# Decoder kernel: norm powers in pairs of batches, transposed outputs copied from separate banks, two steps reordered

## The reference, cut to what matters

```python
x = layernorm(x + L0_attn(x))            # gated delta-rule linear attention, 16 heads of 8
x = layernorm(x + L0_xattn(x, ctx))      # cross attention on a strided gather of keys
x = layernorm(x + L0_ffn(x))             # relu(h + c * sin(theta + 0.1 h)), h = x W1 + b1
x = layernorm(x + L1_attn(x))            # selective scan, 256 channels, 16 states
x = layernorm(x + L1_xattn(ctx, x))      # cross attention, 8 heads of 128
x = layernorm(x + L1_ffn(x))             # receptance-gated feed-forward
```

## Time and profile before

| | before |
|---|---|
| median of 3 runs | 370.88 us (369.8 to 370.9) |
| the profiled execution's own time | 370.45 us |
| its span, first to last instruction | 368.6 us |
| mean granted TensorE clock | 0.952 |
| busy, share of the span: PE, DVE, ACT, POOL | 86%, 81%, 60%, 54% |
| DMA, mean over the span | 66 GB/s |

### The profile page before, as it was taken

One profiled execution on the slowest core, in us unless ns is written; L12 is line 12 of the kernel. 1 busy time (PEld: TensorE's weight loads), 2 busy tenths in 40 slices (PEclk: granted clock), 3 DMA queues, 4 the chain that ended last, 5 costly groups with the idle time before them and its releaser, 6 DMA issues. The chain is left out here.

```text
span 368.6 us, 5671 instructions
## 1 busy us (share of the span) xinstructions
PE 318.2 (86%) x1758; PEld 240.6 (65%) x1758; DVE 300.4 (81%) x739; ACT 222.7 (60%) x511; POOL 200.0 (54%) x236
## 2 busy tenths in 40 slices
PE   5858494997998999888868989898799989999993
PEld 2646393895665647743536955476599668989873
DVE  0798999996977889999999999999958534754945
ACT  4666323233265869887778628888555746775742
POOL 2399997664413141899999899868602800100111
PEclk9989599699999999989996998999999999999999
DMA  8910000000000003345443544444200000000011
GB/s 249 424 57 2 1 0 3 0 1 2 0 2 1 0 2 118 110 136 157 153 133 116 160 128 133 145 140 127 84 2 0 2 0 1 2 1 2 1 30 28
DMA packets 11525, 24.45 MB, mean 66 GB/s; under 512 B 1231, under 2 KB 2255, under 8 KB 11239
## 3 DMA queue, kind: packets, MB, share of 16 engines
q1 hardware_dynamic: 11495, 24.09, 20.0%
HBM read 23.50 MB, written 0.59 MB: 65 GB/s over the span
## 5 line engine op out<-in xcount | busy, mean ns | idle before, releaser
L1064 POOL TENSOR_TENSOR arena<-arena 128x512 f32<-128x512 f32 x63 | 80.0, 1280 | 25.8 <-DVE arena L716 24.0
L716 DVE TENSOR_TENSOR_SCAN arena<-arena,ps 128x512 f32<-128x512 f32 x64 | 77.3, 1209 | 0.1
L1344 ACT ACTIVATE arena<-arena,neg_a 128x508 f32<-128x508 f32 x64 | 43.9, 715 | 6.9 <-DVE arena L716 5.9
L1820 PE MATMUL ps<-first_in,arena 128*128 128x128 f32 x256 | 42.3, 291 | 3.0 <-POOL arena L1064 2.8
L709 DVE TENSOR_TENSOR ps<-arena,ps 128x512 f32<-128x512 f32 x64 | 43.2, 676 | 0.5 <-PE ps L1804 0.5
L1820 PEld LDWEIGHTS ps<-first_in,arena 128*128 128x128 f32 x256 | 33.3, 149 | 14.2 <-POOL arena L1064 8.1
L1110 POOL TENSOR_TENSOR rstd<-veps,mhalf 128x4 f32<-128x4 f32 (+2 forms) x6 | 5.0, 837 | 67.5 <-DVE veps L818 35.5
L744 DVE TENSOR_REDUCE arena<-ps 128x2 f32<-128x496 f32 x32 | 21.3, 667 | 24.8 <-PE ps L1866 24.8
L1804 PE MATMUL ps<-arena,pick_wide 96*128 96x512 bf16 x64 | 25.7, 407 | 12.6 <-DVE arena L716 12.2
L1633 PE MATMUL ps<-arena,first_in 128*128 128x128 f32 (+1 forms) x192 | 26.8, 305 | 8.8 <-POOL arena L941 8.8
L1633 PEld LDWEIGHTS ps<-arena,first_in 128*128 128x128 f32 x192 | 26.1, 219 | 11.0 <-POOL arena L941 10.3
(11 more groups left out here) (300 smaller groups left out, 792.4 us busy)
## 6 DMA issues: line engine op xcount, KB each, us to landing
arena<-c_rows_dram SPq DMA_DIRECT2D x64, 256.0 KB, 3.1
fold_in<-in_fold_dram SPq DMA_DIRECT2D x1, 2056.0 KB, 11.3
late_in<-in_late_dram SPq DMA_DIRECT2D x1, 1423.5 KB, 17.3
early_in<-in_early_dram SPq DMA_DIRECT2D x1, 921.5 KB, 13.1
xres<-in_x_dram SPq DMA_DIRECT2D x1, 512.0 KB, 13.9
kv_ctx<-in_context_dram SPq DMA_DIRECT2D x1, 480.0 KB, 7.1
first_in<-in_first_dram SPq DMA_DIRECT2D x1, 465.0 KB, 3.4
rows_in<-in_rows_dram SPq DMA_DIRECT2D x1, 384.0 KB, 14.4
```

Of the source, the lines that this page charges most:

```text
L716: nc.vector.tensor_tensor_scan(hist[:, q % NBUF], fade[:, q % NFADE], chain(q), 0.0, ALU.mult, ALU.add).then_inc(S("scan"), 1)
L1064: tt(seen[:, q % NBUF], hist[:, q % NBUF], c_wide[:, q % NBUF], ALU.mult).then_inc(S("read_out"), 1)
L1344: act(fade[:, q % NFADE].rearrange("p (b t) -> p b t", t=T)[:, :, 1:], dt[:, n, cols(g)].rearrange("p (b t) -> p b t", t=T)[:, :, 1:], ACT ...
L1820: ins = mm(y_bank(p // NS)[:, b * T:(b + 1) * T], seen[:, p % NBUF, b * T:(b + 1) * T], ident, is_transpose=True, start=False, stop=last a ...
```

## The change

Six edits.

1. In the norms (1, 0), (2, 0), (2, 1) and (3, 0), the list PAIRED, statistics, epsilon and power are done for two batches at a time: two "var" and two "rstd" counts a half, two powers of 128x2 in place of one of 128x4, and `norm_finish` waits for its pair's power.
2. The eight transposes of the linear attention's output go to bank 6 (blocks 0 to 3), bank 7 (4, 5) and bank 5 (6, 7). VectorE copies bank 6, ScalarE banks 7 and 5. All eight turns of `ot` follow when all three copies are in; they go to banks 4 to 7 by pairs of batches, and VectorE copies pairs 0 and 2, ScalarE pairs 1 and 3. `key_rows(0)` moves ahead of `landed(1, 0)`.
3. The subtraction of the maximum and the exponential of the first cross attention are split into two pairs of batches.
4. GpSimd's `power(2, 0)`, `residual_half(3, 0)` and `power(2, 1)` move ahead of the making of `s3_cf`; `power(3, 0)` moves ahead of `residual_half(3, 1)` and its wait.
5. In the sine stage `normal(3, 0, 0)` moves ahead of `last_fraction(1)`; on ScalarE the last block's sine moves behind the two copies to `xcol`.
6. Before the scan VectorE's subtraction for dt (L698) moves ahead of the three instructions for the low bits of B.

```diff
+        PAIRED = [(1, 0), (2, 0), (2, 1), (3, 0)]
+        def o_rows_bank(i):
+            return (bank(6)[:, i * P:(i + 1) * P] if i < 4 else bank(7 if i < 6 else 5)[:, i % 2 * P:(i % 2 + 1) * P])
+        def o_cols_bank(pair):
+            return bank(4 + pair)[:, 0:2 * T]
         def halves(n, g):
-            return ORDER.index((n, g)) + 1
+            at = ORDER.index((n, g)) + 1
+            return at + sum(part in PAIRED for part in ORDER[:at])
+        def pair_count(n, g, i):
+            return halves(n, g) - 1 + i
...
             def landed(n, g, k):
                 ve.wait_ge(S("projected"), (n - 1) * B + (g + 1) * HB)
+                if (n, g) in PAIRED:
+                    for i in range(2):
+                        two = pair_of(g, i)
+                        statistics(two, landing(g, k))
+                        h = slice(two[0], two[-1] + 1)
+                        ts(veps[:, h], mv[:, h, 1], EPS, None, ALU.add).then_inc(S("var"), 1)
+                    return
...
             def norm_finish(n, part, batches, src, dst):
-                ve.wait_ge(S("rstd"), halves(n, part))
                 for b in batches:
+                    if (n, part) in PAIRED and b % 2 == 0:
+                        ve.wait_ge(S("rstd"), pair_count(n, part, b % HB // 2))
+                    elif b == batches[0]:
+                        ve.wait_ge(S("rstd"), halves(n, part))
...
-            ve.wait_ge(S("o_rows_mm"), DH)
-            nc.vector.tensor_copy(ot[:, 0:512].rearrange("p (n i) -> p n i", i=DH),
-                                  bank(6, 2).rearrange("p (i n) -> p n i", i=DH)[:, 0:P // 2]).then_inc(S("o_rows"), 1)
-            ve.wait_ge(S("o_cols_mm"), HB)
-            nc.vector.tensor_copy(otT[:, 0:512], bank(4)).then_inc(S("o_cols"), 1)
+            ve.wait_ge(S("o_rows_mm"), 4)
+            nc.vector.tensor_copy(ot.rearrange("p (n i) -> p n i", i=DH)[:, :, 0:4],
+                                  bank(6).rearrange("p (i n) -> p n i", n=P)).then_inc(S("o_rows"), 1)
+            for g in range(2):
+                ve.wait_ge(S("o_cols_mm"), 4 * g + 2)
+                nc.vector.tensor_copy(otT[:, 512 * g:512 * g + 256], o_cols_bank(2 * g)).then_inc(S("o_cols"), 1)
+            key_rows(0)
             landed(1, 0, 2)
-            key_rows(0)
             normal(1, 0, 2)
...
-                tt(s2e[:, h], sc.rearrange("p b (m h) -> p b m h", h=H), by_head(s2m, g),
-                   ALU.subtract).then_inc(S("score0_shift"), 1)
+                for i in range(2):
+                    two = slice(2 * i, 2 * i + 2)
+                    tt(s2e[:, h][:, two], sc.rearrange("p b (m h) -> p b m h", h=H)[:, two], by_head(s2m, g)[:, two],
+                       ALU.subtract).then_inc(S("score0_shift"), 1)
...
             def gate3(k):
                 ve.wait_ge(S("sine"), k + 1)
+                if k == 0:
+                    ve.wait_ge(S("gate_factor"), 1)
...
             landed(3, 0, 0)
+            normal(3, 0, 0)
             last_fraction(1)
-            normal(3, 0, 0)
             gate3(2)
...
+            ve.wait_ge(S("dt_lost"), 1)
+            ve.wait_ge(S("dt_relu"), 1)
+            then(tt(dt[:, 0, h0], bank(0), dtu[:, 0, h0], ALU.subtract))
             b_left(0).then_inc(S("bc_left"), 1)
...
             b_low(0)
-            ve.wait_ge(S("dt_lost"), 1)
-            ve.wait_ge(S("dt_relu"), 1)
-            then(tt(dt[:, 0, h0], bank(0), dtu[:, 0, h0], ALU.subtract))
...
             def power(n, g):
+                if (n, g) in PAIRED:
+                    for i in range(2):
+                        h = slice(pair_of(g, i)[0], pair_of(g, i)[-1] + 1)
+                        po.wait_ge(S("var"), pair_count(n, g, i))
+                        tt(rstd[:, h], veps[:, h], mhalf[:, h], ALU.pow).then_inc(S("rstd"), 1)
+                    return
...
             residual_half(2, 1, row_in[:, ROWS.index("bo0")])
+            power(2, 0)
+            residual_half(3, 0, row_in[:, ROWS.index("b2")])
+            power(2, 1)
             po.wait_ge(S("theta_sin"), 1)
...
             ts(s3_cf, s3_cf, 0.1, None, ALU.mult).then_inc(S("gate_factor"), 1)
-            power(2, 0)
-            residual_half(3, 0, row_in[:, ROWS.index("b2")])
-            power(2, 1)
+            power(3, 0)
             po.wait_ge(S("projected"), 2 * B + HB)
             residual_half(3, 1, row_in[:, ROWS.index("b2")])
-            power(3, 0)
...
-            ac.wait_ge(S("o_rows"), 1)
-            act(ot[:, 512:].rearrange("p (n i) -> p n i", i=DH),
-                bank(6, 2).rearrange("p (i n) -> p n i", i=DH)[:, P // 2:], ACT.Copy).then_inc(S("o_rows_second"), 1)
-            ac.wait_ge(S("o_cols_mm"), 2 * HB)
-            act(otT[:, 512:], bank(5), ACT.Copy).then_inc(S("o_cols_second"), 1)
+            for i, k in ((4, 7), (6, 5)):
+                ac.wait_ge(S("o_rows_mm"), i + 2)
+                act(ot.rearrange("p (n i) -> p n i", i=DH)[:, :, i:i + 2],
+                    bank(k)[:, 0:2 * P].rearrange("p (i n) -> p n i", i=2), ACT.Copy).then_inc(S("o_rows_second"), 1)
+            for g in range(2):
+                ac.wait_ge(S("o_cols_mm"), 4 * g + 4)
+                act(otT[:, 512 * g + 256:512 * (g + 1)], o_cols_bank(2 * g + 1), ACT.Copy).then_inc(S("o_cols_second"), 1)
...
-                e = s2_e[:, g * HB * NK:(g + 1) * HB * NK]
-                ac.wait_ge(S("score0_shift"), g + 1)
-                act(e, e, ACT.Exp, scale=float(DH) ** -0.5).then_inc(S("exp0"), 1)
+                for i in range(2 * g, 2 * g + 2):
+                    e = s2_e[:, i * 2 * NK:(i + 1) * 2 * NK]
+                    ac.wait_ge(S("score0_shift"), i + 1)
+                    act(e, e, ACT.Exp, scale=float(DH) ** -0.5).then_inc(S("exp0"), 1)
...
             sine(2)
...
+            last_sine(0)
             for m in range(2):
                 ac.wait_ge(S("turned"), 2 * B + 2 * (m + 1))
                 act(xcol[:, 2 * m:2 * m + 2], bank(4 - 3 * m)[:, 0:2 * T].rearrange("p (b t) -> p b t", b=2),
                     ACT.Copy).then_inc(S("xcol"), 1)
+            last_sine(1).then_inc(S("sine"), 1)
...
             def project1(g):
                 for b in range(g * HB, (g + 1) * HB):
+                    if b % 2 == 0:
+                        pe.wait_ge(S("o_cols_second" if b % HB else "o_cols"), g + 1)
...
             pe.wait_ge(S("o_rows"), 1)
+            pe.wait_ge(S("o_rows_second"), 2)
             turn_outputs(0)
-            pe.wait_ge(S("o_rows_second"), 1)
             turn_outputs(1)
-            pe.wait_ge(S("o_cols"), 1)
             project1(0)
-            pe.wait_ge(S("o_cols_second"), 1)
             project1(1)
```

More of the change, by code:

```diff
@@ L156, in normed, with pair_of @@
             return {1: 0, 2: B, 3: 2 * B, 5: 5 * B, 6: 6 * B}[n] + k
+        def o_rows_bank(i):
+            return (bank(6)[:, i * P:(i + 1) * P] if i < 4 else bank(7 if i < 6 else 5)[:, i % 2 * P:(i % 2 + 1) * P])
+        def o_cols_bank(pair):
+            return bank(4 + pair)[:, 0:2 * T]
         def halves(n, g):
-            return ORDER.index((n, g)) + 1
+            at = ORDER.index((n, g)) + 1
+            return at + sum(part in PAIRED for part in ORDER[:at])
+        def pair_of(g, i):
+            return range(g * HB + 2 * i, g * HB + 2 * i + 2)
+        def pair_count(n, g, i):
+            return halves(n, g) - 1 + i
         class Arena:
@@ L610, in shifted @@
                 then(nc.vector.tensor_reduce(s2m[:, h], sc.rearrange("p b (m h) -> p b h m", h=H), AX.X, ALU.max))
-                tt(s2e[:, h], sc.rearrange("p b (m h) -> p b m h", h=H), by_head(s2m, g),
-                   ALU.subtract).then_inc(S("score0_shift"), 1)
+                for i in range(2):
+                    two = slice(2 * i, 2 * i + 2)
+                    tt(s2e[:, h][:, two], sc.rearrange("p b (m h) -> p b m h", h=H)[:, two], by_head(s2m, g)[:, two],
+                       ALU.subtract).then_inc(S("score0_shift"), 1)
             def probabilities(g):
                 h = slice(g * HB, (g + 1) * HB)
-                ve.wait_ge(S("exp0"), g + 1)
+                ve.wait_ge(S("exp0"), 2 * (g + 1))
                 then(nc.vector.tensor_reduce(s2d[:, h], s2e[:, h].rearrange("p b m h -> p b h m"), AX.X, ALU.add))
@@ L1293, in _, with last_sine @@
             sine(2)
-            for m in range(2):
+            def last_sine(m):
+                at = slice(m * 512, (m + 1) * 512)
                 ac.wait_ge(S("fraction"), 4 + m)
-                ins = act(s3_ang[:, 3, m * 512:(m + 1) * 512], s3_ang[:, 3, m * 512:(m + 1) * 512], ACT.Sin, scale=-2 * PI_F)
-            ins.then_inc(S("sine"), 1)
+                return act(s3_ang[:, 3, at], s3_ang[:, 3, at], ACT.Sin, scale=-2 * PI_F)
+            last_sine(0)
             for m in range(2):
@@ L1651, in _ @@
             for i in range(DH):
-                turn(bank(6, 2)[:, i * P:(i + 1) * P], osb[:, i * T:(i + 1) * T], ident).then_inc(S("o_rows_mm"), 1)
```

(7 more changed lines are left out.)

## The result

The kernel after takes 367.7 us (median of 5 runs, 366.57 to 368.32) against 369.8 (5 runs, 369.59 to 370.9): ratio 0.9926, 95% interval 0.9901 to 0.9951, faster by more than the 0.3% that a measurement can tell; the two medians alone give 0.9943. Forecast were 368.1 and a range of 367.0 to 369.6. Measured once more, 6 runs of the kernel after beside 11 of the one before, the medians were 367.66 and 370.48, ratio 0.9924 (0.9899 to 0.9949).

The account below looks back on a forecast made before the run. A relay between engines was taken to set the scan's start, then VectorE bounds the scan and TensorE the tail. Gains summed to 2.51 us: 370.45 - 2.51 = 367.94, plus 0.2, said as 368.1; range 367.0 to 369.6.

Parts of the forecast that it names:

- copies, to TensorE's resuming and to L1705: Linear attention's output: copies split between VectorE and ScalarE let TensorE resume 0.15 us sooner and reach the projection 0.47 sooner.
- pairs in (1, 0): First norm: statistics and powers by two batches, a power of two at 0.76 us, end it 0.62 us sooner.
- split exponential: First cross attention: halving subtraction and exponential gains 0.15 us once; the second half gains nothing.
- pairs in (2, 0): Norm (2, 0): pairs finish earlier, but transposes and next statistics wait for TensorE's project2(1), so gain zero.
- pairs in (2, 1): Norm (2, 1): ends 0.6 us sooner, but ScalarE's copy ahead of the first sine lets only 0.05 pass.
- norm (3, 0) and the order round it: Norm after the sine stage: 3.47 us in pairs instead of 4.13, last_fraction(1) after it still covered; gain 0.62.
- dt order: Before the scan: a ready 0.69 us subtraction fills VectorE's 0.46 idle; gain 0.45, nothing if another input is late.
- equal powers: Rival: GpSimd's power of two costs 1.02 us like four; norm gain 0.22 twice, total 368.9; chance 0.13.
- The cover is exact, with no slack: At norm (3, 0): the late sine and gate3(2) end at 2.5 us, inner(0) at 2.45; up to 0.3 at risk.
- Pairs gain nothing: Rival: VectorE's longer statistics, or the cover at (3, 0), eat both 0.62 gains; total 369.4 us; chance 0.09.
- Slow stores: Rival: ScalarE's two copies into ot take 1.33 us each, losing 1.9; total 370.0, no measurable change; chance 0.08.
- Clock in the tail: Rival: TensorE's granted clock after the scan falls from 0.99 to 0.94, costing 4.8 us; total 372.7; chance 0.04.

Follow-up runs that it names:

- Experiment 6: The kernel after with GpSimd's residual_half(3, 1) moved behind the making of diag_d, waiting for the last fraction: 366.84 us in one execution.
- experiment 1: The kernel before with edit 2 alone (output copies, key rows ahead of the first norm): 369.86 us beside 369.69 for the kernel before.
- experiment 8: The kernel after with the two 128x4 operations behind norm (4, 0)'s statistics, in the scan, done by GpSimd instead of VectorE: 369.75 us.
- trace of 10: The kernel after with GpSimd's residual_half(3, 1) behind the last fraction, timed again: 367.52 us, median of 6 runs, ratio 0.9924.
- 9: The kernel after with residual_half(3, 1) late and the two small scan operations on GpSimd, epsilon behind the hand-over: 368.05 us (4 runs), ratio 0.9932.
- experiment 2: The kernel after with no norm in pairs (PAIRED empty): 368.20 us in one execution.
- experiments 5 and 12: The kernel after with edit 3 undone (whole subtraction and exponential in the first cross attention), executed twice: 367.46 and 368.53 us.
- experiment 7: The kernel after with VectorE's last_fraction(1) ahead of normal(3, 0, 0) again, pairs and the other engines' orders kept: 368.17 us.

## Why the prediction was right, point by point

| term | predicted | measured |
|---|---|---|
| copies, to TensorE's resuming and to L1705 | 0.15 + 0.47 | 0.67 (0.15 + 0.51, rounded) |
| pairs in (1, 0) | 0.62 | 0.66 |
| split exponential | 0.15 | 0.13 |
| pairs in (2, 0) | 0 | 0 |
| pairs in (2, 1) | 0.05 | 0.16 |
| norm (3, 0) and the order round it | 0.62 | 0.38 |
| dt order | 0.45 | 0.42 |
| sum | 2.51 | 2.42 |

Each measured term is the difference between before and after of one stretch from statistic to statistic (the last two: to `inner(0)`, and from there to the scan).

**Copies.** Right, and from where it said. The bound of 1.33 for a copy stored in runs of two is far off: the two took 0.68 together, overlapping, against 0.384 for a contiguous one.

**Pairs in (1, 0).** Right, within 0.04: the power of two was taken by interpolation as 0.76 and took 0.708. The first rival, equal powers, had it at 1.02. It rested on what the Trainium skill, GPSIMD Engine Reference, section 3.1 (Elementwise) states, about 2.6 cycles an element of a two-input operation behind a fixed dispatch. The rows go against it for this operation: from two elements to four it is 0.345 us more, 0.17 an element. For a power the interpolation between the two rows of the trace was the better guide.

**(2, 0).** Right in its reason as well: with and without that pair the relay is the same to 0.01, and TensorE's projection ends the wait.

**(2, 1).** The size was off by 0.11, and the step was mistaken: "the first sine at 119.31 starts 0.10 after ScalarE's copy". It starts when `fraction(0)` ends and overlaps the copy's last tenth, so the copy was no floor under it. In the kernel before, too, `fraction(0)` ended at 119.28, 0.03 ahead of that sine. What held back most of the pair's 0.6 was an input of `fraction(0)`: ScalarE's second angle ends 3.73 behind the first statistic before and after, and VectorE now idles 0.43 for it.

**(3, 0).** This is the term that failed in size, 0.38 for 0.62. The prediction wrote "The cover is exact, with no slack. If it goes, up to 0.3 is lost"; it went. What it had not foreseen is why: it costed `last_fraction(1)` at 1.1 as in the old place, where GpSimd ran only the small power of four (129.54), its residual being done at 129.26, while the new order of edits 4 and 5 puts it beside `residual_half(3, 1)`, which "only `project3(1)` waits for". No engine was waiting for that residual then, and still it costs 0.36 on L690 (0.79 for 0.43). Experiment 6 takes it away and 0.30 comes back. A sign of being wrong that the prediction named did come: the idle time ahead of L1781, now L1824, grew from 0.44 to 0.72.

**dt order.** Right: 0.42, and 0.44 by undoing it alone.

**The scan.** The span fell by 0.6 more than the relay, and nothing shows this as a gain of the change: no edit touches the scan, and experiment 1, with the copies alone, has a scan of 118.65 already. Where the profiled execution shows 1.05 saved, it lies in two gaps (37: 4.43 to 3.92; 41: 2.28 to 1.71), and a second trace of the same kernel shows 0.35. The sentence that a granted clock below 1 in the scan "costs nothing as VectorE bounds it" was wrong. Behind scan 41 of the kernel before VectorE waits for TensorE, whose granted clock was 0.65 from 222 to 225:

```profile
222.91 1.20 DVE L716 TENSOR_TENSOR_SCAN arena<-arena,ps 128x512 f32<-128x512 f32 x1
224.58 0.69 DVE L709 TENSOR_TENSOR ps<-arena,ps 128x512 f32<-128x512 f32 x1 [0.47 <-PE ps L1804]
```

and experiment 8 loses 2.74 to three such waits. A clock fall isn't the only way there: in the trace of 10 the same gap has an idle time of 0.64 at a granted clock of 1.00, so a late hand-over does it too. All traces fit these two. ScalarE's writes of `kv_lat`, released by GpSimd, start 1.13 behind the start of scan 38 in every trace but those of 8, 9 and 10 (2.98, 2.72, 2.14); among the others the gap at 41 is 1.71 wherever the granted clock stayed at 1.00 from 219 to 225, and 2.28 to 2.59 in the three (before, 2 and 12) where it fell. That goes together in each trace; no run here sets the clock by itself. What decides the phase from one execution to the next is open; no run here was made for it.

**The rivals.** *Equal powers*: out, 0.708. *Pairs gain nothing*: out, 1.14 by experiment 2, though at (3, 0), by experiment 7, it would have been right without VectorE's part of edit 5. *Slow stores*: out. *Clock in the tail*: out; the stretch from the last outputs of the scan takes 105.21 for 105.15 at 0.98 for 0.99. The total came out right for the reasons given, with a small help: 370.45 - 2.42 = 368.03 would have been the profiled execution by the relay alone, and it took 367.38. There was some luck in the sum too: (3, 0) gave 0.24 less than its term, and the copies, (1, 0) and (2, 1) together 0.20 more.

## What to carry to other kernels

When an instruction is moved, look at what the *other* engines run at its new place, not only at who waits for whom: a GpSimd sum that nobody was waiting for stretched a VectorE operation from 0.43 to 0.79 and took 0.3 of a gain of 0.7. A stall of a fully busy engine need not be idle time; it can hide in instructions of four elements that take 1.3 us, and moving those away can cost more than it brings if a hand-over to an engine further down comes later for it. Where single executions spread by 1 to 2 us, measure an edit worth tenths by a distance inside the trace, from a fixed start to the instruction that the edit should bring forward.

## What the runs showed of the hardware that was not expected

- **VectorE beside GpSimd.** A 128x512 f32 operation with one tensor input (L690) took 0.43 alone and 0.79 beside GpSimd's 128x512 sum; one of 128x4 took 0.17 with GpSimd idle (L405 at 92.97 before), and behind scan 37 up to 1.32 beside a 128x512 product of 1.27, then ending 0.02 to 0.03 behind that product. The Trainium skill, GPSIMD Engine Reference, section 8 (Key points), says that GpSimd shares its SBUF interfaces with VectorE, with contention for VectorE's instructions in a 2-port mode or with two SBUF inputs. The traces agree that there is contention, and show its size, which for an operation of four elements is all that is left of the other engine's instruction. In which mode L690, L427 and L432 ran, with one tensor input each, no run here shows. Four aggregates beside the same product aren't stretched (0.38), and GpSimd's 128x2 power doesn't stretch L690 (0.43 in experiment 7).
- **The power on GpSimd** takes 0.636, 0.708 and 1.02 to 1.05 us for one, two and four elements: not a straight line, and from two on 0.17 an element.
- **A VectorE start 0.45 after its input**, in both executions of the kernel with the whole exponential (experiments 5 and 12) and in no other trace of the changed kernel. It made edit 3 worth 0.44 rather than 0.13. It isn't explained.
